# Experts' products in three fp32r products of rounded and remainder halves, the weights split on chip during the first stage

## The reference

```
h  = attention(x)           16 heads of 32, 4 key/value heads, rotary on half a head, no mask
x1 = layernorm(x + h)
m  = mlstm(x1, ctx, ctx)    16 heads; decay matrix from input and forget gates; norm by head
x2 = layernorm(x1 + m)
router: logits = x2 @ router_w.T, the best 2 of 16 experts for each token, weights by softmax
expert e: (silu(x2 @ Wu[e]) * (x2 @ Wg[e])) @ Wd[e]    Wu, Wg: 512 x 256, Wd: 256 x 512
shared expert: the same with 512 hidden features
out = layernorm(x2 + shared(x2) + weighted sum over the 2 chosen experts)
```

## Time and profile before

| | |
|---|---|
| time, median of 3 | 2130.97 us |
| profiled execution: time, span | 2131.19 us, 2129.6 us |
| PE busy | 1878.8 us (88%), 11010 instructions |
| DVE busy | 1199.1 us (56%) |
| POOL busy | 693.2 us (33%) |
| ACT busy | 649.3 us (30%) |
| DMA | 226.95 MB, mean 107 GB/s |
| granted clock of TensorE, mean | 0.951 of 2.4 GHz |

### The profile page before, as it was taken

The page is one execution under the profiler, slowest core; times in us unless marked ns, Lnnn a source line. Parts: engine busy times, 40 slices in busy tenths (PEclk is TensorE's granted clock), DMA queues, the critical chain, the costliest instruction groups (busy, mean ns, idle before and its releaser), DMA issues. The chain is left out here.

```text
span 2129.6 us, 35688 instructions
## 1 busy us (share of the span) xinstructions
PE 1878.8 (88%) x11010; PEld 1186.4 (56%) x11011; DVE 1199.1 (56%) x2474; ACT 649.3 (30%) x1358; POOL 693.2 (33%) x754
## 2 busy tenths in 40 slices
PE   3878899998999999898998999998879999999990
PEld 2456565756656575665657566665644454454440
DVE  2567766766776776677667667677442222222225
ACT  0142433324242342424233242423301221221224
POOL 3124132322423232242323224232133444443440
PEclk8889999999999999999999999999889999999995
DMA  7254142334334243343423344332133667656549
GB/s 268 52 116 107 42 117 62 95 88 95 104 67 117 60 97 88 93 109 64 117 60 97 81 95 111 67 97 61 31 144 84 148 149 177 148 120 146 90 74 330
DMA packets 151847, 226.95 MB, mean 107 GB/s; under 512 B 32448, under 2 KB 107200, under 8 KB 149056
## 3 DMA queue, kind: packets, MB, share of 16 engines
q1 hardware_dynamic: 101616, 132.94, 24.2%
q0 software_dynamic: 38336, 92.38, 18.1%
q10 hardware_dynamic: 11792, 0.61, 0.4%
HBM read 94.70 MB, written 48.83 MB: 67 GB/s over the span
## 5 line engine op out<-in xcount | busy, mean ns | idle before, releaser
L1554 PE MATMUL ps<-ug_w,rowsT 128*128 x640 | 292.9, 601 | 7.8 <-SPq L1403 4.6
L1554 PEld LDWEIGHTS ps<-ug_w,rowsT 128*128 128x128 f32 x640 | 122.8, 193 | 164.0 <-issue 164.0
L1443 POOL DMA_INDIRECT sum_rows<-y_sb,pairs x80 | 127.3, 1591 | 248.9 <-DVE y_sb L1521 134.3
L948 DVE SCALAR_TENSOR_TENSOR weighted<-ps,decay 128x384 f32<-128x384 f32 x256 | 140.3, 553 | 84.7 <-PE ps L1169 69.2
L976 DVE RECIPROCAL arden<-ps 128x256 f32<-128x256 f32 x64 | 112.5, 1758 | 133.5 <-PE ps L1300 129.9
L1043 PE MATMUL ps<-wqkv_sb,xT_sb 128*128 128x256 f32 (+1 forms) x512 | 172.7, 491 | 15.6 <-ACT maskr_sb L524 15.6
L1509 DVE SCALAR_TENSOR_TENSOR silu<-tanh,ps 128x256 f32<-128x256 f32 x80 | 33.7, 421 | 251.8 <-ACT tanh L1464 251.8
L931 DVE TENSOR_REDUCE smax<-ps 128x2 f32<-128x512 f32 x256 | 164.3, 682 | 17.1 <-PE ps L1226 16.7
L476 POOL DMA_INDIRECT routed_ids<-pair_w,pos_w x64 | 64.0, 1000 | 328.1 <-DVE pair_w L747 292.5
L641 ACT ACTIVATE probs<-ps 128x1024 f32<-128x1024 f32 x128 | 130.5, 1024 | 108.3 <-PE ps L1277 108.3
L620 ACT ACTIVATE decay<-ps,g_col 128x256 f32<-128x256 f32 x256 | 121.4, 474 | 136.1 <-PE ps L1152 88.7
(11 more groups left out here) (253 smaller groups left out, 3848.6 us busy)
## 6 DMA issues: line engine op xcount, KB each, us to landing
q_stack<-qkT_hi SPq DMA_DIRECT2D x128, 128.0 KB, 3.7
mk_stack<-ctxT_hi SPq DMA_DIRECT2D x128, 128.0 KB, 4.7
mq_stack<-qkT_hi SPq DMA_DIRECT2D x128, 128.0 KB, 2.4
ug_w<-in_expert_ug SPq DMA_DIRECT2D x16, 1024.0 KB, 5.5
xT_sb<-in_xT SPq DMA_DIRECT2D x16, 512.0 KB, 3.3
x_sb<-in_x POOLq DMA_DIRECT2D x16, 512.0 KB, 3.9
ctxT_sb<-in_ctxT POOLq DMA_DIRECT2D x16, 512.0 KB, 3.6
q_stack<-qkT_lo SPq DMA_DIRECT2D x64, 128.0 KB, 4.4
```

What stands on the lines that cost most here:

```text
L948: nc.vector.scalar_tensor_tensor(weighted[:, h % 4, :], ps[:, qk2_bank(h), 0:384], SCALE, decay[:, h % 2, :], ALU.mult, ALU.mult).then_inc ...
L1443: pool.indirect_dma_start(out=sum_dram, out_offset=bass.IndirectOffsetOnAxis(ap=tables.pairs[:, m, 0:1], axis=0), in_=y_sb[:, m % W, :], i ...
L1554: ins = nc.tensor.matmul(ps[:, 2 + k % 2, :], rowsT[:, k % 2, c, :], ug_w[:, bass.ds(slot, 1), c, :].rearrange("p o n -> p (o n)"), start= ...
```

## The change

It has these parts:
1. The experts' up and down products become three fp32r products each (hi*hi, hi*lo, lo*hi), 12 and 6 matmuls of 512 columns per tile in place of 4 and 2 float32 ones.
2. The activations are split per tile: ACT's copy out of PSUM now rounds to fp32r, and DVE subtracts it from PSUM for the remainder (`rest_of_rowsT`, `rest_of_hidT`). PE now turns the rows first in its step and then does up; ACT takes rowsT first.
3. The experts' weights are split on chip: in each of turns 1 to 16 one expert (number y) is cut into 6 pieces of 128x512. SP loads a piece, POOL rounds it (`tensor_copy`) and subtracts (`tensor_tensor`), SP writes both halves to a new DRAM tensor `split_w`. Two pieces are in flight. Pieces 0 and 1 are loaded at the end of the turn before. POOL does pieces 0 to 3 behind its `k_stack` copies and pieces 4 and 5 behind the four indirect DMAs of the routed pairs; SP puts all six between the `q_stack` copies and the maxima's rows.
4. The experts' stage loads 3.1 MB per expert (both halves) instead of 1.5 MB.
5. Room in SBUF: `qk_sb` shares memory with `hid` and `sq` (so ACT's first copy of a turn also waits for `x2_done` of the turn before), the gate weights are 64 columns wide instead of 128, and tiles are allocated in another order.
6. The last stage uses one semaphore where it used three.

```diff
+WCOL = KC * 2 * F + FC * D
+CUT = 512
+CUTS = WCOL // CUT
...
 # first stage, SP
+            def take_cut(e, k):
+                sp.dma_start(cut_lo[:, k % 2, :].bitcast(F32), cut_of(e, k)).then_inc(cut_in[k % 2].sem, 16)
+            def put_cut(e, k):
+                wait(sp, cut_lo_done, e, k + 1)
+                for part, half in enumerate((cut_hi, cut_lo)):
+                    sp.dma_start(split_of(e, part, k), half[:, k % 2, :].bitcast(F32)).then_inc(split_out[k % 2].sem, 16)
+            for k in range(2):
+                take_cut(0, k)
...
                     stack(sp, q_stack, qkT_hi, qkT_lo, None, q_in, Q_ROWS)
-
+                if y is not None:
+                    for k in range(CUTS):
+                        put_cut(y, k)
+                        if k % 2 and k + 1 < CUTS:
+                            for q in range(2):
+                                wait(sp, split_out[q], y, 32 * (k // 2 + 1))
+                                take_cut(y, k + 1 + q)
+                if b is not None:
                     wait(sp, m_hi_done, b, 1)
...
                     stack(sp, mk_stack, ctxT_hi, ctxT_lo, None, mk_in, K_ROWS)
+                if y is not None and b is not None:
+                    for q in range(2):
+                        wait(sp, split_out[q], y, split_out[q].per)
+                        take_cut(y + 1, q)
...
 # first stage, POOL
+                def split(k):
+                    wait(pool, cut_in[k % 2], y, 16 * (k // 2 + 1), rest=rest)
+                    nc.gpsimd.tensor_copy(cut_hi[:, k % 2, :], cut_lo[:, k % 2, :].bitcast(F32)).then_inc(cut_hi_done.sem, 1)
+                    wait(pool, cut_hi_done, y, k + 1, rest=rest)
+                    nc.gpsimd.tensor_tensor(cut_lo[:, k % 2, :], cut_lo[:, k % 2, :].bitcast(F32), cut_hi[:, k % 2, :].bitcast(F32),
+                                            ALU.subtract).then_inc(cut_lo_done.sem, 1)
+                if y is not None:
+                    for k in range(CUTS - 2):
+                        split(k)
                 if w is not None:
                     wait(pool, pairs_done, w, 1, rest=rest)
...
+                if y is not None:
+                    for k in range(CUTS - 2, CUTS):
+                        split(k)
...
 # experts' stage, SP
-                sp.dma_start(ug_w[:, s, :, :].rearrange("p c f -> p (c f)"), expert_ug[e]).then_inc(w_in[s], 16)
-                sp.dma_start(d_w[:, s, :, :].rearrange("p c d -> p (c d)"), expert_d[e]).then_inc(w_in[s], 16)
+                for part in range(2):
+                    sp.dma_start(split_w[:, s, part, :].bitcast(F32), split_dram[e, :, part, :]).then_inc(w_in[s], 16)
...
 # experts' stage, DVE
+            def rest_of_rowsT(m, k):
+                dve.wait_ge(rowsT_hi_done, m + 1)
...
+                v.tensor_tensor(rowsT_lo[:, k % 2, :, :], ps[:, k % 2, :].rearrange("p (c r) -> p c r", r=P),
+                                rowsT_hi[:, k % 2, :, :].bitcast(F32), ALU.subtract).then_inc(rowsT_lo_done, 1)
...
 # experts' stage, PE
                 for c in range(KC):
-                    ins = nc.tensor.matmul(ps[:, 2 + k % 2, :], rowsT[:, k % 2, c, :],
-                                           ug_w[:, bass.ds(slot, 1), c, :].rearrange("p o n -> p (o n)"),
-                                           start=c == 0, stop=c == KC - 1)
+                    for i, (rT, part) in enumerate(((rowsT_hi, 0), (rowsT_hi, 1), (rowsT_lo, 0))):
+                        ins = nc.tensor.matmul(ps[:, 2 + k % 2, :], rT[:, k % 2, c, :],
+                                               split_w[:, bass.ds(slot, 1), part, 2 * F * c:2 * F * c + 2 * F].rearrange("p o n -> p (o n)"),
+                                               start=c + i == 0, stop=c + i == KC + 1)
...
             def step(n, k, landed):
+                if has(n, 0):
+                    transpose_rows(n, k, landed)
                 if has(n, 1):
                     up(n - 1, k - 1)
                 if has(n, 2):
                     transpose_hidden(n - 2, k - 2)
-                if has(n, 0):
-                    transpose_rows(n, k, landed)
                 if has(n, 3):
                     down(n - 3, k - 3)
```

More of the change, by code:

```diff
@@ L44 @@
 W = 4
-Tables = namedtuple("Tables", "id_sb idx pairs row0 turns weights slot ends pairs_in base_out base_last ready free_at down_read all_added")
+WCOL = KC * 2 * F + FC * D
+CUT = 512
+CUTS = WCOL // CUT
+Tables = namedtuple("Tables", "id_sb idx pairs row0 turns weights slot ends pairs_in base_out base_last ready free_at down_read all_added split_out")
 class Signal:
@@ L204, in attention_and_mlstm @@
         mrden = sb("mrden", [P, ST, H])
-        hid = sb("hid", [P, ST, H, HD])
-        sq = sb("sq", [P, ST, H, HD])
+        cut_hi = sb("cut_hi", [P, 2, CUT], F32R)
+        cut_lo = sb("cut_lo", [P, 2, CUT], F32R)
+        hid_sq = sb("hid_sq", [P, 2, ST * H * HD])
+        hid, sq = (hid_sq[:, q, :].rearrange("p (t h d) -> p t h d", h=H, d=HD) for q in range(2))
+        qk_sb = hid_sq[:, :, :].rearrange("p a n -> p (a n)")[:, 2 * QKH * ROT:2 * QKH * ROT + ST * QKH * HD]\
+            .rearrange("p (t h d) -> p t h d", h=QKH, d=HD)
         hid_flat = hid[:, :, :, :].rearrange("p t h d -> p (t h d)")
@@ L307, in attention_and_mlstm @@
         sd_ready, base_done = sig("sd_ready", ST), tables.down_read
+        cut_in = [sig(f"cut_in{q}", CUTS // 2 * 16) for q in range(2)]
+        cut_hi_done, cut_lo_done = sig("cut_hi_done", CUTS), sig("cut_lo_done", CUTS)
+        split_out = tables.split_out
         x_v = x.rearrange("(b t p) d -> b p t d", t=ST, p=P)
@@ L316, in one, with cut_of, split_of @@
             return v[b] if isinstance(b, int) else v[bass.ds(b, 1)].rearrange("o p t d -> (o p) t d")
+        def cut_of(e, k):
+            v, k = (expert_ug, k) if k < KC else (expert_d, k - KC)
+            cols = slice(CUT * k, CUT * k + CUT)
+            return v[e, :, cols] if isinstance(e, int) else v[bass.ds(e, 1), :, cols].rearrange("o p n -> (o p) n")
+        def split_of(e, part, k):
+            cols = slice(CUT * k, CUT * k + CUT)
+            if isinstance(e, int):
+                return split_dram[e, :, part, cols]
+            return split_dram[bass.ds(e, 1), :, part, cols].rearrange("o p n -> (o p) n")
         FIRST_S, MAXIMA_AT = 6, 6 + H // 2
@@ L535, in pass_through @@
                         wait(act, av_pair, b, 0)
+                        if w is not None:
+                            wait(act, x2_done, w, ST)
                     qkv = ps[:, 2 * t:2 * t + 2, :].rearrange("p a n -> p (a n)")
@@ L1405, in _ @@
             wait(sp, tables.free_at, B - 1, PAIRS)
+            for q in range(2):
+                wait(sp, tables.split_out[q], B - 1, tables.split_out[q].per)
             for e in range(W):
@@ L1572, in down @@
                 for f in range(FC):
-                    ins = nc.tensor.matmul(ps[:, 4 + k % 2, :], hidT[:, k % 2, f, :],
-                                           d_w[:, bass.ds(slot, 1), f, :].rearrange("p o d -> p (o d)"),
-                                           start=f == 0, stop=f == FC - 1)
+                    for i, (hT, part) in enumerate(((hidT_hi, 0), (hidT_hi, 1), (hidT_lo, 0))):
+                        of_f = slice(2 * F * KC + D * f, 2 * F * KC + D * f + D)
+                        ins = nc.tensor.matmul(ps[:, 4 + k % 2, :], hT[:, k % 2, f, :],
+                                               split_w[:, bass.ds(slot, 1), part, of_f].rearrange("p o d -> p (o d)"),
+                                               start=f + i == 0, stop=f + i == FC + 1)
                 ins.then_inc(down_ready, 1)
             def step(n, k, landed):
+                if has(n, 0):
+                    transpose_rows(n, k, landed)
                 if has(n, 1):
@@ L1668, in measure @@
                     ins = v.bn_aggr(mv[:, n, :], stats[:, n, :])
-                ins.then_inc(aggregated, 1)
-                dve.wait_ge(aggregated, g + 1)
-                v.tensor_scalar(var[:, G * g:G * g + G], mv[:, G * g:G * g + G, 1], LN_EPS, None, ALU.add).then_inc(var_done, 1)
+                step(ins)
+                v.tensor_scalar(var[:, G * g:G * g + G], mv[:, G * g:G * g + G, 1], LN_EPS, None, ALU.add).then_inc(measured, 1)
+                n_steps[0] += 1
+                assert n_steps[0] == PER_GROUP * g + OF_VAR
             def scale(g):
```

84 lines of the change are left out of this document (50 added, 34 removed).

## The result

The change makes the kernel slower. After the change the median is 2179.53 us (four runs, 2176.19 to 2182.48), beside 2132.18 us (four runs) for the kernel before on the same chip: ratio 1.0223, 95% interval 1.0198 to 1.0248. Forecast were 2088 us, range 2045 to 2140. The span went from 2129.6 to 2179.0 us, +49.4.

The account below looks back on a forecast made before the run. The prediction took PE, 88% busy, to bound the kernel. From 2131 us it took 91 for faster products and added 15 for doubled weight loads and 33 for the first stage's split: 2088 us, range 2045 to 2140.

Parts of the forecast that it names:

- upper bound of 45: Experts' stage, doubled weight loads: +45 us at most, if adds waiting for each other stretch with queue load throughout.
- upper bound of 0.24: Experts' products: at most 0.24 us per 512-column fp32r product, scaled up from the 384-column product's pitch.
- Rival 3: Experts' products: 0.42 us each, not one column per clock or weight loads not hidden; 2357 us, chance 0.04.
- (a): First stage, pieces 0 and 1: POOL's work holds DVE's gate chain, +1 us per turn behind the slack.
- (b): First stage, pieces 2 and 3: POOL's work meets DVE's small SBUF operations placing the routed rows, +0.7 us per turn.
- (c): First stage, pieces 4 and 5: piece 5's writes still in SP's queue before the maxima's rows, +0.5 us per turn.
- Rival 1: First stage: SP sends the maxima's rows late because piece 5 goes first; 2145 us at 6 us per turn, chance 0.17.
- Rival 2: Experts' stage: adds and weights bound all of it, a tile 5.3 us instead of 4.67; 2123 us, chance 0.14.
- Rival 4: Both stages: the splits find only slack and the loads are covered; 2050 us, chance 0.13.

Follow-up runs that it names:

- e3: The changed kernel with each expert's weight load starting one tile later; ratio 1.0335 to the kernel before.
- e8: The changed kernel with adds trailing gathers by 7 tiles instead of 5 and ACT fetching the pair lists earlier in its step; ratio 0.9950 to the kernel before.
- e12: e8 without loading the remainder halves of the experts' weights; one execution, 2088.46 us beside 2107.16 for the kernel before.
- e1: The changed kernel without loading the weights' remainder halves, their products taking the rounded halves again; ratio 1.0193 to the kernel before.
- e9: The changed kernel with the old order in a step (up, hidden turned, rows turned, down); ratio 1.0249 to the kernel before.
- e2: The changed kernel without the first stage's split, each expert's unsplit weights loaded twice; ratio 1.0049 to the kernel before.
- e10: e8 with the split's pieces moved later in the turn and SP sending the maxima's rows before the last pieces; ratio 0.9863 to the kernel before.
- e11: e8 without POOL's rounding and subtraction, all DMAs of the pieces kept; ratio 0.9784 to the kernel before.
- b1: The kernel before, unchanged, run again for its profile on another chip; 2120.08 us.

## Why the prediction was wrong

The sum of the span's change, by the same terms: products -77, experts' rows and weights +88 (forecast +15), first stage +37 (forecast +33), together +48 of the 49.4 measured. The first is 79 x (5.81 - 4.84); the second is L 469.9 less 79 x 4.84 = 382, 88 us of waiting and of products at the lower clock (the granted clock from 1640 to 2050 is 0.91, before 1.00; no run takes the two apart), where before 457.9 less 79 x 5.81 leaves none.

**Part 4 is the step that failed: "from 1725 to 1820 ... becomes one of DMA, +18", I take +15.** I added up DMA busy time per stretch and compared it with PE's time, as if the transfers could use any moment of the stretch. The stretch did not fill: from 1725 to 1820 the DMA share rose only from 0.72 to 0.74, and in the same part of the stage, which now lies 37 us later, to 0.78; PE still fell to 78 and 73 of 95 us busy (length, busy of PE, its weight loads, DVE, ACT and POOL, then clock, DMA share and GB/s, as in the earlier trace rows).

```profile
1725.00:1820.00 95.00, 78.07 (x357) 61.38 (x355) 39.08 (x75) 17.94 (x44) 38.82 (x30) 0.93 0.74 199
1762.00:1857.00 95.00, 72.69 (x312) 56.74 (x311) 33.94 (x65) 16.06 (x39) 33.42 (x26) 0.87 0.78 237
```

What decides is the latency of one gather against its lead, and the lead comes from a loop: scaling of tile n-6, add, gather of n, landing, transposes of n. From that scaling to the transposes the median was 14.9 us before and is 10.1 after. Where nothing waits it is 9.2 to 9.4, of which 3.5 pass before the gather is issued; that leaves some 5.8 us for a landing that takes 4.3 in the median and up to 10 beside a load (`e3`). Two parts of the change shortened it, and I priced neither there: each tile is 1 us shorter, and PE turns the rows at the head of its step instead of behind up. The loads, twice as long, then lengthen the landing, POOL's order passes the delay on to the next gather, and PE works on at half the clock. `e8` and `e12` take the 88 us apart: 63 by the lead, 28 by the traffic (together 91, since these runs come from other chips). The shares hang on the order: with the lead as it was, half the traffic is worth 35 us (`e1`), and the lead then the other 55.
The upper bound of 45 was built on the same error: the adds' waiting "over the whole stage" as DMA busy time, not as a hold on the gathers behind them. I had the row for it: an add that waits 7.2 us for an earlier one, with a gather behind it.

**Part 1, the products**, was right in kind: 0.213 us of the pitch is 512 columns at one per clock of 2.4 GHz, and loads of 204 ns are hidden under it. The size was off, 0.238 us for up (0.248 for down) and not 0.223, 4.84 and not 4.67 for a tile, 14 us in all; the transposes, 0.49 us and not 0.66 a tile, gave back half of what the products took more. The upper bound of 0.24, from the 384-column product, was the right row. Rival 3 is refuted.

**Part 2, the activations' halves**: 0 as forecast in the changed order; `e9` shows what the new order hides, 0.5 us per quiet tile. That order was the right choice and also what cost the rows their lead.

**Part 3, the split in the first stage**: mechanism right, size too small. I had 2.2 us per turn; it is 2.5 between the two profiles (93.31 to 95.82) and 3.2 between kernels of one chip (`e1`, `e2`). Over the ten turns it is 3.4 (93.43 to 96.85); the last turns take less. Means over them, against the profile of before: from the last gate product to the first decay product +0.7 (forecast 1.0 for (a), of which 1.65 us more in DVE's four operations, as forecast), from there to the fifth weighting +1.1 (0.7 for (b)), from there to the first product with the maxima +1.2 (0.5 for (c)), 3.0 in all. Part of it is a term that I did not have: behind the new waits the granted clock falls. In the turn shown, PE after, from 1085 to 1105 us:

```profile
1085.00:1095.00 10.00, 8.26 (x66) 0.83 0.65 214
1095.00:1105.00 10.00, 9.55 (x70) 0.83 0.36 116
```

And PE before, in the same part of the turn:

```profile
1055.00:1065.00 10.00, 8.75 (x78) 1.00 0.20 36
1065.00:1075.00 10.00, 9.42 (x88) 1.00 0.01 0
```

Over the ten turns the clock from 10 to 20 us behind the first decay product is 0.77, before 0.97; in `e10`, where POOL keeps out of the gate chain, and in `e11`, without its operations, it is 1.00. `e11` shows that (c), SP and its queue, is nothing. What is left is POOL, and it costs by holding DVE: from 300 to 1500 us no engine waits longer for POOL than before, but DVE's operations on small SBUF tiles are longer, 2.8 us per turn, 1.65 of them in the gate chain and 1.2 where the rows are placed. The Trainium skill, page "SBUF — State Buffer", section "SBUF: two separate sides", says that GpSimd and a VectorE operation with two inputs in SBUF take one pair of ports in turn, each for its whole instruction. This trace agrees: 1.50 us for L965, with two such inputs, beside a subtraction of 1.26, against 0.47 alone.
**Parts 5 and 6**: 0 as forecast. `e2` has them without the split, and its L0 of 1607.2 is that of the kernel before (`b1`, 1607.6). From the last scaling to the end it is 53.2 us, before 52.7.

**The rivals.** Rival 1 (SP late with the maxima's rows): in the turn shown SP issues its last copy 2.9 us before it sends m_hi, and `e11` finds no cost in SP's DMAs, so no. Rival 2 (a tile of 5.3, bound by adds and weights) had the right place but a throughput in it, and its 5.3 has no sum behind it (339 us in 80 tiles are 4.2); the stage came out at 5.95 per tile with quiet tiles of 4.84. Rival 4 (only slack is used) fell with both.

Open: why L0 of the kernel before is 1619.0 in one profile and 1607.6 on another chip at the same mean clock. The profiles show where, not why: over ten turns the lowest clock of a turn, 0.77 and 0.75, lies 25 to 30 us behind the first decay product in the first and 30 to 35 in the second, and the way from that product to the maxima takes 30.7 and 28.9 us. Open too: what the lower clock alone costs in each stage, since no run has the waits without it.

## What to carry to other kernels

When an engine gets faster, look for the loops that run through it, and measure for each prefetch the time from its issue to its use, beside its longest landing under load: the lead is counted in steps of the faster engine and shrinks with them. A prefetch that stands in one engine's program behind an operation that waits has that wait in its latency; more distance between the two is a change of one number. On-chip preparation on POOL was paid for by DVE here: put it where DVE reads PSUM or has slack, not into a chain of small SBUF operations.

## What I had not expected of the hardware

- A wait costs twice: behind 6.35 us without rows PE ran at a granted clock of 0.50 for at least 5.5 us, with products 0.43 us apart instead of 0.238.
- A gather of 128 rows lands 4.3 us after its issue (median of 56 in `e3`, at most 5.5) while no weights are loaded, and 8.5 us after it (24 gathers, at most 10.0) beside loads of 3.1 MB per expert; an add held the next one up by 9.27 us.
- Small waits count as well: behind a wait of 0.67 us in the first stage the granted clock was 0.83 over 20 us, though PE was over 80% busy there; before, without that wait, it was 1.00.
- The kernel before differs by up to 1% between chips (medians 2112.3 to 2133.7). The changed kernel was timed on two, both with the kernel before at 2132 to 2134, and has 1.0223 and 1.0235 there; `e3`, with the same experts' stage (470.3), has nearly the same time (2185.85) on a chip where the kernel before has 2112.3, and so 1.0335. A ratio from one chip carries 1% of its own.
